# Dequantisation, all batches and the stores of the last stage in one block

## The reference

```python
def _dequant_fp4(packed_i32, scales_f16, group_size):
    nib = w[:, :, None] >> shifts & jnp.uint32(15)
    vals = _FP4_LUT[nib.astype(jnp.int32)].reshape(out_f, in_p * 8)
    return vals * s_full

gate_up = jnp.einsum('bsh,oh->bso', x, w_gu)          # 512 inputs, 2 x 1408 outputs
gate, up = (gate_up[..., :I], gate_up[..., I:])
h = jax.nn.silu(gate) * up
y = jnp.einsum('bsi,hi->bsh', h, w_down)              # back to 512
rms = jnp.sqrt(jnp.mean(y * y, axis=-1, keepdims=True) + EPS)
return y / rms
...
x = x + _L1_ffn_ref(_layernorm(x, axis=-1), ...)
```

## Time and profile before

| | before |
|---|---|
| median of 3 runs | 2084.62 us |
| profiled execution | 2088.46 us |
| its span | 2086.6 us |
| TensorE matmuls busy | 1601.1 us (77%) |
| VectorE busy | 1412.8 us (68%) |
| ScalarE busy | 873.7 us (42%) |
| GpSimd busy | 625.0 us (30%) |
| last stage, from its first instruction to the end of the span | 1650.2 to 2086.6 us |

### The profile page before, as it was taken

How to read it: one execution, slowest core, us unless ns; L and a number is a source line. 1 busy time by engine, 2 the same in 40 slices (tenths; PEclk the granted TensorE clock), 3 DMA queues, 4 the chain that set the end, 5 groups by cost and what they waited for, 6 DMA issues and landing times. The chain is left out here.

```text
span 2086.6 us, 20794 instructions
## 1 busy us (share of the span) xinstructions
PE 1601.1 (77%) x6523; PEld 650.2 (31%) x6523; DVE 1412.8 (68%) x2163; ACT 873.7 (42%) x1125; POOL 625.0 (30%) x402
## 2 busy tenths in 40 slices
PE   4778886976651486289988988998899539898995
PEld 2232332432220232142244225323532213333332
DVE  3598898989986353558747855783687479655552
ACT  1546444463330110144643654364456234544452
POOL 0364555646635326130022003000300014242332
PEclk9898898988995799598999999999999769999998
DMA  4343444544557552400000000000000350000002
GB/s 154 102 140 111 134 129 115 141 117 134 143 125 174 142 101 77 161 1 1 2 11 1 2 12 1 1 1 12 1 1 1 78 117 0 1 1 0 0 1 81
DMA packets 65665, 131.77 MB, mean 63 GB/s; under 512 B 11536, under 2 KB 11792, under 8 KB 64800
## 3 DMA queue, kind: packets, MB, share of 16 engines
q1 hardware_dynamic: 49552, 94.73, 15.9%
q0 software_dynamic: 7168, 25.19, 5.4%
q10 hardware_dynamic: 8848, 10.58, 1.8%
HBM read 134.13 MB, written 12.87 MB: 70 GB/s over the span
## 5 line engine op out<-in xcount | busy, mean ns | idle before, releaser
L313 POOL TENSOR_TENSOR ssm_dBu<-ssm_du,ssm_BC 128x1024 f32<-128x1024 f32 x128 | 301.0, 2353 | 283.4 <-DVE ssm_du L328 107.4
L378 DVE TENSOR_TENSOR_SCAN ssm_dA<-ssm_dA,ssm_dBu 128x512 f32<-128x512 f32 x256 | 312.1, 1220 | 12.7 <-ACT ssm_dA L286 10.2
L223 PE MATMUL ssm_psY<-ssm_hC,ident 128*128 128x512 f32 x512 | 265.2, 645 | 69.6 <-DVE ssm_hC L335 69.4
L286 ACT ACTIVATE ssm_dA<-ssm_delta,ssm_negA 128x512 f32<-128x512 f32 x256 | 175.6, 692 | 271.4 <-DVE ssm_hC L335 271.2
L1186 DVE TENSOR_REDUCE soft_next_mx<-soft_next_psS 128x1 f32<-128x512 f32 x384 | 248.1, 686 | 50.8 <-PE soft_next_psS L1074 48.4
L1232 ACT ACTIVATE soft_next_Pr<-soft_next_psT 128x1024 f32<-128x1024 f32 x192 | 189.1, 1020 | 114.1 <-PE soft_next_psT L1101 113.9
L1449 DVE SCALAR_TENSOR_TENSOR mlp_first<-mlp_psQ,mlp_s_gu,mlp_first 128x512 f32<-128x512 f32 x176 | 131.9, 749 | 128.0 <-ACT mlp_first L1485 118.2
L1507 POOL TENSOR_TENSOR mlp_both<-mlp_first,mlp_third 128x512 f32<-128x512 f32 x88 | 125.3, 1424 | 283.3 <-DVE mlp_first L1449 143.1
L987 POOL TENSOR_TENSOR att_QS<-att_rot,att_QS 128x1024 f16<-128x1024 f32 x16 | 34.1, 2129 | 508.9 <-ACT att_QS L976 508.9
L335 DVE TENSOR_TENSOR ssm_hC<-ssm_dA,ssm_BC 128x512 f32<-128x512 f32 x256 | 172.7, 675 | 20.2 <-PE ssm_psY L223 20.2
L1534 PE MATMUL mlp_psD<-mlp_Wd,mlp_hT 128*128 128x512 f32 x352 | 170.7, 630 | 10.3 <-DVE mlp_hT L1430 10.3
(11 more groups left out here) (278 smaller groups left out, 2258.2 us busy)
## 6 DMA issues: line engine op xcount, KB each, us to landing
ssm_BC<-bc_rows SPq DMA_DIRECT2D x128, 512.0 KB, 4.8
moe_W<-in_masksT POOLq DMA_DIRECT2D x32, 512.0 KB, 9.1
deq_words<-in_gate_upT SPq DMA_DIRECT2D x32, 176.0 KB, 14.0
moe_XP<-sorted_rows ACTq DMA_DIRECT2D x4, 1030.0 KB, 22.7
X<-in_x SPq DMA_DIRECT2D x4, 1024.0 KB, 14.8
moe_XP<-results SPq DMA_DIRECT2D x4, 1024.0 KB, 9.0
out_x<-X SPq DMA_DIRECT2D x1, 4096.0 KB, 12.5
mlp_Wd<-in_downT ACTq DMA_DIRECT2D x8, 352.0 KB, 19.1
```

The costliest lines, as they stand in the source:

```text
L223: nc.tensor.matmul(psY[:, w, :], ident[:], hC[:, q % RC, :], start=False, stop=(n == DS - 1)).then_inc(summed, 1)
L286: nc.scalar.activation(dA[:, q % RA, :], delta[:, b % 2, e, :], ACT.Exp, scale=negA[:, e, n:n + 1]).then_inc(dA_done, 1)
L313: nc.gpsimd.tensor_tensor(dBu[:, g % RB], du[:, b % 2, hh * W:(hh + 1) * W, :], BC[:, g % RING, 0, :].unsqueeze(1).broadcast_to([P, W, S]) ...
L378: nc.vector.tensor_tensor_scan(dA[:, q % RA, :], dA[:, q % RA, :], dBu[:, g % RB, w, :], 0.0, ALU.mult, ALU.add).then_inc(h_done, 1)
```

## The change

All of the last stage, from the decoding to the stores, stands in one block with counters that run on through the batches; nothing is cleared between, and no engine meets another except through these counters. The loop over batches 1 and 2 is written out. Beside that:

- The row statistics are computed for four tiles at a time: those of batch 0 at the start, those of batch b + 1 ahead of the even unit's sums of pass 3 of batch b. ScalarE takes their root in pass 4.
- The gate and up codes are decoded in place in `words`, with one helper buffer, and TensorE's first unit waits for the four chunks of Vgu one by one.
- On VectorE in batch 0, the decoding of a down tile (`down_weights`) stands behind the even unit's sums and ahead of `gated`, where it stood ahead of these sums.
- SP stores each batch as soon as its four tiles are added, in four DMAs of 1 MB instead of one of 4 MB.

```diff
+        with nc.Block() as block:
+            @block.sync
+            def _(sp):
...
+                for b in range(B):
+                    sp.wait_ge(added, NT * (b + 1))
+                    sp.dma_start(out4[:, b], X4[:, b]).then_inc(stored, 16)
+                sp.wait_ge(stored, 16 * B)
...
+                def unit(b, u):
+                    U = b * UNITS + u
...
+                    if u == 0:
+                        pe.wait_ge(xh_done, NT * (b + 1))
+                        pe.wait_ge(xl_done, NT * (b + 1))
+                    for g in range(DT):
+                        if U == 0:
+                            pe.wait_ge(gu_done, g + 1)
+                        elif u >= 1:
+                            pe.wait_ge(ev_v if g % 2 else ev_a, 2 * (U - 1) + g // 2 + 1)
...
+                turn(0)
+                for b in range(B):
+                    for j in range(JT):
+                        unit(b, 2 * j)
+                        unit(b, 2 * j + 1)
+                        if j >= 1:
+                            down_product(b, j - 1)
+                    if b + 1 < B:
+                        turn(b + 1)
+                    down_product(b, JT - 1)
...
+                        if b + 1 < B and u == JT - 3:
+                            root_variances(b + 1)
...
+                for g in range(DT):
+                    dve.wait_ge(chunk_in[g], 16 * PER)
+                    codes(words[:, g, :], words[:, g, :], sign[:]).then_inc(vals, 1)
...
+                for b in range(B):
+                    for u in range(UNITS):
+                        U = b * UNITS + u
+                        j, w = divmod(u, 2)
+                        if u == JT - 5 and b + 1 < B:
+                            row_stats(b + 1)
+                        if u == JT and b + 1 < B:
+                            normalise(b + 1)
                         row = w * JT + j
                         for n, g in enumerate((1, 3)):
-                            dve.wait_ge(grp, DT * u + g + 1)
+                            dve.wait_ge(grp, DT * U + g + 1)
...
+                        if b == 0 and w == 0:
+                            down_weights(j)
+                        if b >= 1 and u == 1:
+                            mean_squares(b - 1)
+                        if b >= 1 and u == 2:
+                            add_results(b - 1)
                         if w == 0 and j >= 1:
-                            gated(j - 1)
-                    gated(JT - 1)
-                    if nb is not None:
-                        low_parts(dve)
+                            gated(b * JT + j - 1)
...
-        run(0, 1, None)
-        with nc.Fori(1, B - 1) as b:
-            run(b, b + 1, b - 1)
-        run(B - 1, None, B - 2)
-        run(None, None, B - 1)
...
-        stage_mlp(nc, X, ident, ins)
-        with nc.Block() as block:
-            @block.sync
-            def _(sp):
-                sp.dma_start(out.rearrange("b (t p) d -> p (b t) d", p=P), X[:]).then_inc(stored, 16)
-                sp.wait_ge(stored, 16)
+        stage_mlp(nc, X, ident, stored, ins, out)
```

More of the change, by code:

```diff
@@ L1284, in stage_mlp @@
         xl = sb("xl", [P, DT, S], F16)
[L1285 to L1295, removed]
@@ L1298, in normalise @@
[L1298 to L1307, removed]
@@ L1309, in high_parts @@
[L1309 to L1319, removed]
@@ L1395, in stage_mlp @@
         ss = sb("ss", [P, NT])
+        psQ = m_.ps("psQ", [P, DT, S])
         psD = m_.ps("psD", [P, NT, D])
[L1397 to L1418, removed]
-                    if b is None:
-                        mean_squares()
-                        add_results()
-                        return
-                    def gated(j):
-                        dve.wait_ge(silu_done, j + 1)
-                        dve.wait_ge(summed, 2 * j + 2)
-                        if j >= 3:
-                            dve.wait_ge(down, j - 2)
-                        nc.vector.tensor_tensor(hT[:, j % 3, :], sg[:, j % 2, :], both[:, 1, :], ALU.mult).then_inc(h_done, 1)
-                    for u in range(2 * JT):
-                        if u == JT and nb is not None:
-                            normalise(nb)
-                        j, w = divmod(u, 2)
-                        if first_batch and w == 0:
-                            chain.link(codes(chain, Wd[:, j, :].bitcast(I32), td[0][:], td[1][:]))
-                            half = td[0][:].bitcast(F16).rearrange("p (o w) -> p o w", w=2)[:, :, 0]
-                            nc.vector.scalar_tensor_tensor(out=Wd[:, j, :], in0=half, scalar=2.0 ** 14, in1=s_d[:, j, :],
-                                                           op0=ALU.mult, op1=ALU.mult).then_inc(wd_done, 1)
@@ L1499, in _ @@
-                @block.gpsimd
-                def _(pool):
-                    for u in range(2 * JT if b is not None else 0):
-                        j, w = divmod(u, 2)
-                        pool.wait_ge(ev_a, 2 * u + 2)
-                        pool.wait_ge(ev_v, 2 * u + 2)
-                        if j >= 1:
-                            pool.wait_ge(h_done if w else silu_done, j)
-                        nc.gpsimd.tensor_tensor(both[:, w, :], first[:, w, :], third[:, w, :], ALU.add).then_inc(summed, 1)
@@ L1546 @@
+                    gated(b * JT + JT - 1)
+                    if b + 1 < B:
+                        low_parts(b + 1)
+                mean_squares(B - 1)
+                add_results(B - 1)
 LAYOUT = {
```

247 lines of the change are left out of this document (174 added, 73 removed).

## The result

The changed kernel takes 2115.57 us (median of 4 runs, 2113.63 to 2120.65) against 2085.16 us for the kernel before beside it (4 runs, 2084.57 to 2085.86): 30.4 us more, a ratio of 1.0149 with a 95% interval of 1.0130 to 1.0169. The prediction was 2106.5 us with a range of 2089 to 2114. The direction and the place are as forecast, the size is not: the time lies 1.6 us above the range. The profiled execution took 2120.65 us, the longest of the four, with a span of 2118.9 us, 32.3 more than the 2086.6 before.

What follows compares the result with a forecast made beforehand. TensorE was taken to set the pace in batches 1 to 3, with VectorE nearly full in batch 0. Terms summed to +6.5 without the clock and +21.9 with it, giving 2106.5 us on the median, range 2089 to 2114.

Steps and rivals of the forecast that it cites:

- Step (1): Batch 0, passes 2 to 10: down decoding ahead of the gated product makes passes 10.57 instead of 7.22 us, +30.2.
- The rival in which the chain hides: Batch 0: the decoding chain costs nothing and the change does only what it removes, 2060.9 us; chance 0.03.
- Step (2): Batch 0: the normalisation now falls beside down matmuls and no longer delays a pass, -4.1 us.
- Step (3): Start of batch 0, one block from decoding on: fewer statistics and in-place decoding save 0, pass 2 starts 2.9 us earlier.
- Steps (4) and (5): Three changes of block between batches go, -5.7 us; at the end, block changes and a smaller last store, -11.0 together.
- Step (7): Row statistics per batch, ahead of the sums of pass 3: cost 0, with a bound of +2 us in all.
- Step (6): Batch 0: TensorE's idle ahead of down groups lowers its clock in 8 of 10 passes, +15.4 us, bounds 0 and 26.5.
- every idle falls: Batch 0: every down group starts at the slow clock, 10 x 1.93 = 19.3 us, so 2110.4; chance 0.20.
- dearer still: Clock falls cost 2.65 us each, statistics are blocked, instructions come late: 2115 us and more; chance 0.06.
- The lock is escaped: Batch 0: L1294 gets ahead of GpSimd's sum, the chain is 2.46 us, 2081.7 without a clock fall; chance 0.06.

Runs made afterwards that it cites:

- e3_filler: The changed kernel with 14 matmuls whose results nobody reads filling TensorE's wait in passes 1 to 10 of batch 0: 2092.97 us.
- e1_old_place: The changed kernel with the down weights decoded ahead of the even unit's sums again, as in the kernel before: 2065.16 us, ratio 0.9899 to the kernel before.
- e7_stats_first: The changed kernel with the down decoding in its old place and the row statistics of all four batches at the start: 2064.89 us.
- e2_order_alone: The kernel before with one edit, the down weights decoded behind the even unit's sums and ahead of the gated product: 2136.32 us.
- e5_one_store: The changed kernel with the down decoding in its old place and a single 4 MB store at the end: 2072.91 us.
- e4_pool_waits: The changed kernel with GpSimd's sum of the even unit in batch 0 waiting until that pass's down weights are decoded: 2089.24 us.

## Why the prediction was right or wrong

- **Step (1), the chain ahead of the gated product: right.** With the clock kept (e3_filler) a pass is 10.53 where 10.57 was forecast, and L1446 keeps 1.37. The rival in which the chain hides gave 2060.9. e1_old_place, in which it does hide, took 2065.16, so the price of the order without the clock is 21.6 + 6.2 = 27.8, against 30.2 - 4.1 = 26.1. The 27.8 hold ten chains and the forecast nine. Like for like, from the start of pass 2 to the transposes, e3_filler takes 95.5 us (1716.86 to 1812.32) and the kernel before 69.1: 26.3 more.
- **Step (2), the normalisation hidden: right.** L1465 starts at 1766.47 beside a down group, and the next down group's idle is 3.30 like all others.
- **Step (3), the start: half right.** Statistics for fewer tiles saved nothing, as said, and e7_stats_first shows the same from the other side. But the fourth chunk is waited for until 41.7 us behind the first issue instead of 40.4, which with a stage start 0.3 later makes the 1.6. The hand-drawn start of pass 2 at 1715.8, plus 1.6, plus 2.9 for a slow first down group (6.60), gives 1720.3, and it is at 1720.34. The ten kernels that decode in place all have this wait at 41.4 to 42.2, the two with buffers of their own (before, e2_order_alone) at 40.4 and 41.0. Whether decoding in place slows the transfers is not shown by that; it stays open.
- **Steps (4) and (5), the changes of batch and the end: right.** Behind batch 0 the sum was -5.7 - 11.0 = -16.7, and the traces have -17.8. Of that, 0.8 is no gain of the change: the slow groups in pass 1 of batches 1 to 3 took 5.9 us over 3.70 together in the one execution and 5.1 in the other. The store alone was put at -8.2, and e5_one_store has 8.4; a store of 1 MB was put at 4.3 us and took 4.2.
- **Step (7), row statistics at nothing: right.** They lie beside down matmuls, and a GpSimd sum beside them doesn't lengthen them (2.46 alone at the start of the stage as well). In the order of e1_old_place the same edit costs 1.8 in batch 0. The cover came from the idle that step (1) made.
- **Step (6), the clock: the term that was mis-sized.** It was put at 8 falls of 1.93, +15.4. The runs have 24.2 (the changed kernel against e3_filler) and the trace 25.3: ten falls of 2.53 on average. Two errors went the same way: 2 falls more at 1.93 are 3.9 us, and 0.6 more for each of ten is 6.0. "At 8 of 10 passes" leaned on idles of 2 us that keep the clock, when the idle in question, 3.3, was of the length of the earlier trace rows, and both of those fell, as did the third of its kind at 1808.10 (5.40). Three rows could not tell 8 from 10; the 27 of 36 of the later traces would have spoken for 8, and why the clock fell at every one of those that come back each pass is open. Nor do idles of 2 us or less always keep the clock: before, in pass 1 of batch 0, idles of 1.14 us (ahead of 1710.07) and 1.60 us (ahead of 1712.27) with 0.6 us of matmuls between them were followed by 0.50 and a down group of 4.45 (1714.41). And the mean of three extras was taken as the price, with 1.51 and 1.63 in it: seven of the ten took 2.86 to 3.07 extra, above the dearest seen before. The clock was at 0.50 for nearly all of each of the seven, where it came back or fell on the way in the other three. The bound of 26.5 (ten at 2.65) was nearly reached, so the case was foreseen, at a price 6 us too low.

The account of batch 0, forecast terms for what went as forecast and measured ones for the chunk and the clock, closes: 30.2 - 4.1 - 2.9 = 23.2 without the clock, 1.6 for the chunk and 25.3 for the clock make 50.1, and the transposes of batch 1 start 50.1 us later.

The rule of the Trainium skill that the prediction weighed ("TensorE: Matmul & The Clock Gate", section "HAM oscillation — how this bites in real kernels", a loop that waits between its bursts starts each of them at the low clock) holds for nine of the ten bursts of the changed kernel; the tenth, at 1766.40, starts at 1.00 and falls on the way, and is slow as well. The sum by it, 2110.4, took the same 1.93 for a fall and was still 5.2 short of the median. The page's loop waits some 3 to 5 us. At the shorter idles here four bursts of ten were slow at 2.35 us and none at 1.8.

Of the rivals, "every idle falls" is what happened, at 2.53 a fall, near the 2.65 of "dearer still". "The lock is escaped" didn't occur by itself, and e4_pool_waits shows that it was worth more than was reckoned (2081.7 with a high clock throughout): its 9.4 us are real, but four groups still fell. Without their 6.7 us its 2089.24 would be 2082.5.

## What to carry to other kernels

An in-order engine that feeds another must do first what the other waits for: 3.3 us of decoding that had been free beside the down matmuls cost 28 us in ten passes once it stood ahead of the gated product. An idle of TensorE has a second price behind the first, so look at how long the group behind it takes and not only at the wait; here the second was as large again (24 us). Splitting a change by its parts is worth the runs: the order lost some 50 us, the rest gained 21, and the rest with the statistics at the start and one more wait on GpSimd gained 1.2%.

## What the runs showed of the hardware

- An idle of 3.3 us that came back ahead of each group of eight fp32 matmuls was followed by a slow group 20 times of 20 (changed kernel, e2_order_alone). Single idles of 3.34 to 3.48 us in pass 1 of batches 1 to 3 were so in 27 of 36 cases over the twelve traces. One of 2.65 us did it once in eight in the profiled execution, one of 2.35 four times in ten, eight of 1.79 and those of 0.3 never. In the kernel before, a fall followed two idles of 1.14 and 1.60 us close together. At the same length the clock falls or stays, and the runs don't show what decides.
- A slow group in batch 0 took 5.1 to 5.4 us or 6.6 to 6.8 instead of 3.70, depending on how much of it ran at 0.50 (4.36 once, in e7_stats_first, where f16 matmuls ahead of it bore a part). I had expected one price.
- Matmuls whose results nobody reads kept the clock in all ten waits, and cost nothing that shows where TensorE would wait: 24.2 us less with fourteen in each of ten waits, the same within 1 us with seven.
- VectorE's second decoding instruction (int32, a mask and a shift of 128x512) takes 0.43 us alone and 1.37 beside a GpSimd sum that started ahead of it; the row statistics (four of 128x512 in 2.46 us) take the same with a GpSimd sum beside them.
- A store of 1 MB lands in 4.2 us (the median of four) and one of 4 MB in 12.5. A straight line through the two leaves 1.4 us fixed, an estimate near the 1.6 that the prediction had from the earlier trace rows.
